# Second attention of a decoder layer: values kept transposed, sums inverted by way of DRAM, weighed on GpSimd, packed for the output product by DMA

## What is computed

```python
def _L0_xattn_ref(x, cross_input, ...):        # H = 16 heads of D = 16
    ...
    y = einsum('bhqk,bhkd->bhqd', softmax(att), v)          # causal, over x
    y = y + einsum('bhqk,bhkd->bhqd', softmax(attc), vc)    # over the context
    y = y.transpose(0, 2, 1, 3).reshape(B, T, C)
    return y @ Wp + bp
```

## Time and profile before

| | |
|---|---|
| median of 3 runs | 1285.73 us (1284.77 to 1291.07) |
| the profiled execution's own time | 1284.18 us |
| its span, first to last instruction | 1282.5 us |
| TensorE busy | 1180.3 us, 92% |
| VectorE busy | 924.3 us, 72% |
| ScalarE busy | 821.3 us, 64% |
| GpSimd busy | 499.1 us, 39% |
| mean granted TensorE clock | 0.982 |

### The profile page before, as it was taken

How to read it: one execution, slowest core, us unless ns; L and a number is a source line. 1 busy time by engine, 2 the same in 40 slices (tenths; PEclk the granted TensorE clock), 3 DMA queues, 4 the chain that set the end, 5 groups by cost and what they waited for, 6 DMA issues and landing times.

```text
span 1282.5 us, 25128 instructions
## 1 busy us (share of the span) xinstructions
PE 1180.3 (92%) x8870; PEld 535.9 (42%) x8870; DVE 924.3 (72%) x2376; ACT 821.3 (64%) x1577; POOL 499.1 (39%) x519
## 2 busy tenths in 40 slices
PE   6799999999999999868899988888888999999998
PEld 2233434444444444234333233322333266666666
DVE  3777777777777777767788787778877467656564
ACT  3566666666666666634677766676666677667663
POOL 0267878888777788914212111131111130000000
PEclk9999999999999999988999999999999899999999
DMA  7534333322333332021121221112100522232300
GB/s 226 169 101 120 101 83 94 99 81 80 82 83 84 84 81 83 12 71 42 48 80 43 65 61 42 43 53 72 42 26 1 197 97 102 80 135 100 115 17 17
DMA packets 82482, 103.00 MB, mean 80 GB/s; under 512 B 12626, under 2 KB 74066, under 8 KB 82326
## 3 DMA queue, kind: packets, MB, share of 16 engines
q1 hardware_dynamic: 81174, 100.87, 26.9%
q10 hardware_dynamic: 160, 0.39, 0.1%
q0 software_dynamic: 1024, 0.13, 0.1%
HBM read 65.37 MB, written 10.68 MB: 59 GB/s over the span
## 4 chain that ended last, share of the span: by engine, by line
PE 75%; DVE 14%; ACT 5%; issue 4%; DMA 1%; POOL 1%; ACTq 0%; SPq 0%; DVEq 0%; POOLq 0%
PE a_s L1301 10%; PE a_o L466 9%; DVE a_mx L1609 8%; PE a_m L1287 7%; PE a_o L1220 6%; PE a_a L409 6%; PE a_s L456 5%; PE a_s L457 4%; PE a_m L1175 4%; PE a_e L506 3%; PE a_a L419 3%; PE a_m L432 3%; PE a_a L166 3%; PE a_s L1202 3%; PE a_s L1287 2%
## 5 line engine op out<-in xcount | busy, mean ns | idle before, releaser
L1609 DVE TENSOR_REDUCE a_mx<-a_m 128x1 f32<-128x512 f32 (+3 forms) x512 | 271.4, 583 | 77.7 <-PE a_m L1175 68.6
L1434 ACT ACTIVATE a_pt<-a_s 128x512 f32<-128x512 f32 (+3 forms) x512 | 235.0, 515 | 113.9 <-PE a_s L1202 111.5
L637 ACT ACTIVATE a_pt<-a_s 128x512 f32<-128x512 f32 x256 | 149.6, 597 | 167.0 <-DVE a_s L764 138.7
L755 DVE CUSTOM_DVE_ANT_0 a_junk<-a_m,a_rtile 128x512 f16<-128x512 f32 x256 | 167.2, 687 | 0.7 <-issue 0.7
L846 POOL TENSOR_TENSOR a_ps<-a_ps,a_pt 128x512 f32<-128x512 f32 x128 | 159.6, 1268 | 1.0 <-ACT a_pt L637 1.0
L466 PE MATMUL a_o<-a_pt,a_v 128*64 128x512 f32 x512 | 140.0, 625 | 2.6 <-DVE a_a L769 2.5
L1855 POOL TENSOR_SCALAR_AFFINE_SELECT a_pt<-a_pt 128x512 f32<-128x512 f32 x64 | 40.8, 637 | 226.5 <-ACT a_pt L1434 226.5
L764 DVE TENSOR_TENSOR a_s<-a_s,a_near 128x218 f32<-128x218 f32 (+1 forms) x256 | 107.9, 433 | 14.5 <-PE a_s L457 11.6
L456 PE MATMUL a_s<-a_q,a_k 128*128 128x512 f16 x256 | 99.2, 388 | 7.6 <-ACT a_pt L637 6.2
L744 DVE TENSOR_TENSOR a_nat<-a_a,a_nat 128x512 f16<-128x512 f32 x64 | 44.3, 692 | 83.7 <-ACT a_nat L612 83.7
L846 POOL TENSOR_TENSOR a_ps<-a_pt 128x512 f32<-128x512 f32 x64 | 80.0, 1270 | 55.5 <-ACT a_pt L637 55.5
(11 more groups left out here) (295 smaller groups left out, 2606.5 us busy)
## 6 DMA issues: line engine op xcount, KB each, us to landing
a_rtile<-lines SPq DMA_DIRECT2D x32, 448.0 KB, 3.9
a_q<-a_nat SPq DMA_DIRECT2D x192, 64.0 KB
a_k<-a_nat SPq DMA_DIRECT2D x192, 64.0 KB
a_vy<-in_Wa SPq DMA_DIRECT2D x12, 1024.0 KB, 4.9
a_vy<-in_Wb SPq DMA_DIRECT2D x12, 1024.0 KB, 7.3
a_qk<-halves SPq DMA_DIRECT2D x40, 128.0 KB, 2.7
halves<-a_held SPq DMA_DIRECT2D x16, 256.0 KB, 2.3
halves<-a_held SPq DMA_DIRECT2D x32, 128.0 KB, 2.4
```

The source lines that it names most:

```text
L637: act.activation(pt[:, n % RING, ::-1], bank_s[j % 2][:, :], ACT.Exp, scale=SC1 / QS).then_inc(sm["act_s"], 1)
L755: dve.tensor_tensor_reduce(junk[h][:, :], bank_m[h][:, :], rtile[:, u % 3, h, qb * P:qb * P + S], -1 / MAXROW, 3e38, ALU.add, ALU.min, mx[ ...
L1434: act.activation(pt[g % 4][:, h, first:], bank_s[(32 * u + j) % 3][:, first:], ACT.Exp, scale=SC2 / QS).then_inc(sm["act_s"], 1)
L1609: dve.tensor_reduce(mx[u % 2][:, qb, to:to + 1], bank_m[j % 3][:, 0:keys], AX.X, ALU.max).then_inc(sm["dve_b"], 1)
```

## The change

The copy of the bank stays transposed all the way. Each unit's eight rows of sums (4 heads, 2 halves, 512 queries) go to DRAM (`sums2`), come back as 128 x 32 (`total_of`), are inverted by one VectorE instruction, go to DRAM again (`inverses2`) and come back spread, each row of 512 to 32 partitions (`inv`). GpSimd then multiplies the two halves, adds them and adds the bias: four instructions of 128 x 512. Four DMAs pack the 64 value rows of the unit into `yts`. The two transposes and their copies are gone. SP carries these DMAs for units 0 to 14 and POOL those of unit 15. Buffers: `osb` three deep, `y`, `ys`, `r` gone.

```diff
-        CROSS, SELF, MAX, ROWS_AT, SCORE, VALUE, COPY, TURN, ADD = -13, -9, 16, 33, 38, 42, (49, 57), (61, 63), 64
+        CROSS, SELF, MAX, ROWS_AT, SCORE, VALUE, COPY, INVERT, WEIGH = -13, -9, 16, 33, 38, 42, (49, 57), 64, 70
+        OPS = 4
...
+        def of_unit(u, name, n=1):
+            return (sm[f"last_{name}"], n * DMA) if u == UNITS - 1 else (sm[name], n * DMA * (u + 1))
+        flat_row = [[2 * G2 * S // P, P], [1, 2 * G2 * S // P]]
+        def gather(engine, u):
+            if u < 0:
+                return
+            engine.wait_ge(sm["act_o"], 2 * u + 2)
+            for x in range(2):
+                engine.dma_start(sums2[u, x], osb[u % 3][x][D2:P:2 * D2, :]).then_inc(of_unit(u, "sums_out")[0], DMA)
+            engine.wait_ge(*of_unit(u, "sums_out", 2))
+            if u > 0:
+                engine.wait_ge(sm["dve_r"], u)
+            engine.dma_start(total_of[:, :], bass.AP(sums2.tensor, u * 2 * G2 * S, flat_row)).then_inc(of_unit(u, "sums_in")[0], DMA)
+        def spread_inverse(engine, u):
+            if u < 0:
+                return
+            engine.wait_ge(sm["dve_r"], u + 1)
+            engine.dma_start(bass.AP(inverses2.tensor, u * 2 * G2 * S, flat_row), inv_of[:, :]).then_inc(of_unit(u, "inv_out")[0], DMA)
+            engine.wait_ge(*of_unit(u, "inv_out"))
+            if u > 0:
+                engine.wait_ge(sm["pool_y"], OPS * u)
+            for x in range(2):
+                engine.dma_start(inv[x][:, :], bass.AP(inverses2.tensor, (2 * u + x) * G2 * S, [[S, G2], [0, 2 * D2], [1, S]])
+                                 ).then_inc(of_unit(u, "inv_in")[0], DMA)
+        def pack(engine, u):
+            if u < 0:
+                return
+            b, g = divmod(u, GROUPS)
...
+            if u > 0:
+                engine.wait_ge(*of_unit(u - 1, "packed", G2))
+            engine.wait_ge(sm["pool_y"], OPS * u + OPS)
+            for h in range(G2):
+                o = g % 2 * CG + h * D2
+                engine.dma_start(yts[b][o:o + D2, g // 2, :], osb[u % 3][0][h * 2 * D2:h * 2 * D2 + D2, :]
+                                 ).then_inc(of_unit(u, "packed")[0], DMA)
 
         def sync(sp):
...
                 store_self(sp, second, halves2, u)
+                gather(sp, u - 4)
+                pack(sp, u - 5)
+                spread_inverse(sp, u - 4)
...
+            for u in range(UNITS - 4, UNITS - 2):
+                gather(sp, u)
+                pack(sp, u - 1)
+                spread_inverse(sp, u)
             sp.wait_ge(sm["pe_o"], 8 * (UNITS - GROUPS))
-            sp.wait_ge(ps["act_y"], KC * (LATE + 1))
             for u in range(UNITS_E):
                 i = u % 2
+                if u == 2:
+                    gather(sp, UNITS - 2)
+                    pack(sp, UNITS - 3)
+                    spread_inverse(sp, UNITS - 2)
+                if u == 3:
+                    pack(sp, UNITS - 2)
...
             def product_y(b, i, to):
-                pe.wait_ge(ps["act_y"], KC * (b + 1))
+                pe.wait_ge(*of_unit(b * GROUPS + GROUPS - 1 - b // (B - 1), "packed", G2))
+                if b == B - 1:
+                    pe.wait_ge(*of_unit(UNITS - 1, "packed", G2))
...
-                    if (slot, n) == (2, 4):
-                        pe.wait_ge(sm["dve_y"], 2 * UNITS)
-                        turn_y(LAST, 0, bank_a)
-                    if (slot, n) == (2, 5):
-                        turn_y(LAST, 1, bank_o)
-                    if (slot, n) == (2, 8):
+                    if (slot, n) == (3, 1):
+                        pe.wait_ge(sm["act_rows"], UNITS)
                         product_y(LAST, 0, bank_a)
-                    if (slot, n) == (2, 9):
+                    if (slot, n) == (3, 2):
                         product_y(LAST, 1, bank_o)
...
             def out_of_bank(u, x):
                 act.wait_ge(sm["pe_o"], 8 * u + 4 * x + 4)
-                if u > 0:
-                    act.wait_ge(sm["pe_t"], 2 * u + x - 1)
-                act.activation(osb[x][:, :], bank_o[:, :], ACT.Copy).then_inc(sm["act_o"], 1)
+                if u > 2:
+                    act.wait_ge(*of_unit(u - 3, "packed", G2))
+                act.activation(osb[u % 3][x][:, :], bank_o[:, :], ACT.Copy).then_inc(sm["act_o"], 1)
...
-            def weigh(u, x):
...
+            def invert(u):
+                dve.wait_ge(*of_unit(u, "sums_in"))
                 if u > 0:
-                    dve.wait_ge(sm["pool_y"], u)
...
+                    dve.wait_ge(*of_unit(u - 1, "inv_out"))
+                dve.reciprocal(inv_of[:, :], total_of[:, :]).then_inc(sm["dve_r"], 1)
...
+                    if (slot, n) == (2, 6):
+                        invert(UNITS - 1)
...
+            def weigh(u, step):
+                o = osb[u % 3]
+                pool.wait_ge(*of_unit(u, "inv_in", 2))
+                if step < 2:
+                    ins = pool.tensor_tensor(o[step][:, :], o[step][:, :], inv[step][:, :], ALU.mult)
+                else:
+                    pool.wait_ge(sm["pool_y"], OPS * u + step)
...
+                    if step == 2:
+                        ins = pool.tensor_tensor(o[0][:, :], o[0][:, :], o[1][:, :], ALU.add)
+                    else:
+                        ins = pool.tensor_scalar(o[0][:, :], o[0][:, :], vb[:, u % GROUPS:u % GROUPS + 1], None, ALU.add)
+                ins.then_inc(sm["pool_y"], 1)
...
+                u, i = unit_at(n, WEIGH, 2 * OPS)
+                if u is not None and u < UNITS - 1 and i % 2 == 0:
+                    weigh(u, i // 2)
...
+            gather(pool, UNITS - 1)
+            spread_inverse(pool, UNITS - 1)
+            for step in range(OPS):
+                weigh(UNITS - 1, step)
+            pack(pool, UNITS - 1)
```

More of the change, by code:

```diff
@@ L999, in order_of_bank_a @@
             for n in CLOCK:
-                for x in range(2):
-                    u, i = unit_at(n, TURN[x])
-                    if u is not None:
-                        yield "turn", 2 * u + x
                 for name, first, least in (("cross", CROSS, 2), ("self", SELF, 1), ("rows", ROWS_AT, 0)):
@@ L1035, in attention_2_and_experts @@
         before = dict(zip(uses[1:], uses))
[L1036 to L1037 removed]
+        emptied = {"cross": sm["dve_cross"], "self": sm["dve_self"], "rows": sm["act_rows"],
+                   "product": ps["dve_w"], "turn x": ps["dve_lo"]}
         def bank_a_free(pe, name, i):
@@ L1315, in tensor @@
                     make(n - FILL)
-                for x in range(2):
-                    u, i = unit_at(n, TURN[x])
-                    if u is not None:
-                        turn_back(u, x)
                 u, i = unit_at(n, CROSS, 2)
@@ L1768, in vector @@
                     make(n - FILL)
-                for x in range(2):
-                    u, i = unit_at(n, TURN[x])
-                    if u is not None:
-                        weigh(u, x)
+                u, i = unit_at(n, INVERT)
+                if u is not None and u < UNITS - 1:
+                    invert(u)
                 u, i = unit_at(n, SELF + 2)
```

105 lines of the change are left out of this document (33 added, 72 removed).

## The result

The changed kernel takes 1328.35 us (median of 4 runs, 1325.08 to 1332.04) against 1287.1 us for the kernel before on the same chip: a ratio of 1.032, 95% interval 1.028 to 1.036. The profiled execution took 1326.7 us, its span is 1325.0 us, 42.5 us more than before. I had forecast 1288 with a range up to 1306: the time lies outside it, on the slow side.

A forecast was written before the change was run, and what follows sets the result against it. TensorE and VectorE were taken to alternate in the attention and TensorE alone to bound the expert stage: 1284.2 - 14 + 17 = 1287.2, with the median 1.5 us above the profiled execution, given as 1288; range 1271 to 1306.

The forecast's parts named there:

- The gain of the removed work: Attention: transposes, reciprocals and products removed, less a new reciprocal, leave 15.6 us, taken as 14; ends 7 and 20.
- I charge nothing in the steady state: Attention units: the spread lands in 3 to 7 us, GpSimd's triangle is ready in time, so no cost.
- rival 2: Attention: the spread lands late in every unit, `pv` waits about 2 us 15 times, 30 us, 1318 in all; chance 0.13.
- the turns as pure cost: Attention: two `turn_back` of four transposes a unit removed from TensorE, 1.4 us a unit, 6.8 us on the chain.
- Rival 4: Something else, as a clock falling in more places because TensorE has gaps; either side, no size given; chance 0.05.
- the loss at the passage, 17 us: Passage to the experts: 15.4 us of hole in TensorE's list and 1.6 us of clock restart; ends 10.4 and 26.
- The hole before the last product: Expert stage: values packed at 1051 against a product able to start at 1035.6, 15.4 us; sign 12 to 22 us.
- Its cover: SP in each attention unit: free at 908.5, next work the moves at 915.34, so 7 us cover the added wait.
- the units were to be 0.9 us shorter: Attention, sign in the profile after: distance between VectorE's once-a-unit rows shorter by about 0.9 us; wrong if units keep their length.
- Rival 1: Passage to the experts: the tail is hidden, packing ends near 1037, only the steady gain is left, 1273; chance 0.17.
- Rival 3: Attention: TensorE's wait for banks replaces the transposes, only 4 us come out, 1299 in all; chance 0.15.

The follow-up runs named there:

- e1: The changed kernel with the spread as eight transfers of 32 outermost rows in place of two: 1316.16 us, ratio 1.024 to the kernel before.
- e8: The changed kernel with the spread as eight transfers and eight unused transposes a unit where the removed ones stood: 1299.82 us, ratio 1.011 to the kernel before.
- e9: The changed kernel with e1, e4 and e8 together (wide spread, later last product, unused transposes): 1272.02 us, ratio 0.989 to the kernel before.
- e5: The kernel before with only the spread added, as two narrow transfers into a buffer that nobody reads: 1290.64 us, ratio 1.005.
- e11: The changed kernel, its spread left narrow, with the eight unused transposes a unit of e8: 1323.79 us, ratio 1.028 to the kernel before.
- e7: The kernel before with one of four blocks transposed in each turn of the attention's output, no transfer added: 1298.65 us, ratio 1.012.
- e10: The changed kernel with e1 and e4 together, without the unused transposes: 1292.91 us, ratio 1.005 to the kernel before.
- e4: The changed kernel with the last product one slot later in the expert stage, unit 15's inversion and what follows moved too: 1305.16 us, ratio 1.016 to the kernel before.
- e13: e10 with eight unused transposes a unit in one row ahead of the self projection: 1303.68 us, ratio 1.015 to the kernel before.
- e6: The kernel before with only the spread added, as eight transfers of 32 outermost rows into an unread buffer: 1286.43 us, ratio 1.000.

## Why the prediction was wrong

**The gain of the removed work had about the right size; its terms were not those that I gave.** I took 14 us out, ends 7 and 20, which is 0.9 us a unit. Where the clock is full and the spread wide, the units are 1.0 us shorter (140.5 to 134.3 us for six, e1), and over the attention e8 is 11.7 us shorter, e9 11.6. But `turn_back` had 6.8 of my 18.1 us by its share of the chain, and e8, which has the transposes on TensorE again, is as fast in these units as e1 without them. What TensorE no longer did was worth nothing there; the gain came of the rest of the turn. That the total fits is in part luck.

**First failed step: "I charge nothing in the steady state".** It rested on the spread's landing of 3 to 7 us. It measures 8.0 to 10.4. I had the bound from transfers with many partitions on both sides and had the Trainium skill's rule against it beside me; I used the rule only to choose the end of the range. And I looked for the victim in the wrong place. I followed the spread to its own readers, as rival 2 did: GpSimd's multiplication, the triangle, `pv`. GpSimd's multiplications do wait (76 us in all between 640 and 1020), and nothing follows from it: `pv`'s weight loads wait 2.6 us in all for the triangle, and waited 2.7 before. The one that waits is score, 8.3 us in weight loads, for a 4 KB transfer issued by another engine 0.6 us behind the spread. The prediction lists what is queued behind every new wait on an engine, and not what shares the DMA engines with the new transfer. This is worth 12 us as the kernel stands (e1), 6 in the kernel before (e5), 24 with the unused transposes in (e8, e11).

**Second failed step: the turns as pure cost.** "Each unit loses two `turn_back`" was priced by what TensorE no longer does. What it also no longer does is be at work among its short waits. Rival 4 named it, a clock that falls in more places because TensorE has gaps, and gave it 0.05 and no price. Measured alone (e7) three quarters of the removal cost 14 us; in the changed kernel with the spread wide, all of it costs 16 us (e8 against e1), or 21 with the tail mended (e9 against e10). The row was there to be read: in the earlier trace rows TensorE had 14 of 100 us idle at 0.97, and the earlier trace rows showed the clock at 0.50. I took that as a matter of the passage.

**Third failed step: the loss at the passage, 17 us, measures 30.5.** The hole before the last product was forecast as 15.4 us, 17 with the clock. It measures 19.05 us, within the 12 to 22 that I gave as a sign, and its place and releaser are as told. What I put at nothing are two more places: `turn_x` waits 6.5 us for GpSimd's scaling, and `downward` 3.3 us for a `low` that stands behind `invert` of unit 15: with the hole 28.9 of the 30.5 us. The hole itself fits because two delays nearly cancel: TensorE reaches the product at 1049, not 1035.6, and the last values are packed at 1068.1, not 1051. Of the 17 us of the packing, 12.3 are the late second copy of unit 14. Of the rest, two terms were too short: GpSimd weighs unit 14 beside VectorE's splits in 8.2 us, not 5.6 (the multiplications 1.7 us each, the addition 2.07, the bias 2.33), and the spread of unit 15 is in 10 us after its issue, not 3 to 7. Unit 15's weighing took the 5.6 us that were its lower bound. Moving the product by one slot takes 23 us off (e4), 23 with the spread wide (e10 against e1) and 28 with the unused transposes (e9 against e8).

**Smaller terms.** `invert` takes 0.345 us, not 0.25, within the bounds; it waits 3.2 us for unit 15 as well as 11.5 for unit 14. GpSimd's bias addition takes 1.56 us (1.8 taken). SyncE has ten new issues a unit, not thirteen (three in `gather`, three in `spread_inverse`, four in `pack`). Its cover was misread: its next work behind the spread is not the moves at 915.34 but, in every second unit, a store of the context's halves, which the kernel before has at

```profile
912.26 1.23 SPq L181 DMA_DIRECT2D halves<-a_held  x2
```

so 4 us were there by my layout and not 7. They were enough: in the unit shown SyncE had issued the spread by 912.2 and made this store at 916.97. And 1287.2 with 1.5 us to the median is 1288.7, which I wrote as 1288.

**The signs and the rivals.** The hole came; but the units were to be 0.9 us shorter, and they are 0.7 us longer in the mean (386.6 against 376.1 us for 15): one of my signs of being wrong. Rival 1, a hidden tail, did not come. Rival 2 had the landing (its threshold was 9 us, the median is 9.2) and the wrong victim. Rival 3, an alternation that is not relieved, is refuted by the six units at full clock. What made the result was rival 4 with rival 2's transfer, and a passage with more places than I had.

What stays open: why the clock falls at some of these waits and not at others of the same length (up to its eighth once-a-unit row e1 has a clock of 1.00, without the transposes), and which of the things that went with the turns gives the 1.0 us a unit.

## What to carry to other kernels

Before taking work from TensorE, look at what stands between its waits: work that fills gaps may cost nothing and hold the clock up (e8), and the same work at the one other place that was tried was a loss (e13). A new large transfer has to be looked at beside every small one that is in flight at the same moment on any queue, and its outermost dimension kept large on both sides: 32 rows cost nothing here where 4 did (e5, e6). Where a chain of transfers is added ahead of an in-order consumer, move the consumer by the whole chain, measured with the queue that it will find there.

## What the runs showed that I had not expected

- Eight unused transposes a unit, 112 in all with 19.6 us of busy time in e8, make the kernel 16 to 21 us faster (e8 against e1, e9 against e10).
- At full clock these transposes cost nothing: six units take 134.3 us with them and without.
- A single wait of 1.5 us of TensorE was followed by 10 us at the 1.2 GHz level.
- A transfer of 4 KB on GpSimd's queue took up to 5.4 us to land beside transfers of 256 KB with four outermost rows on SyncE's, against 3.3 us at most before.
- The changed kernel with three edits, a wide spread, a later last product and the unused transposes, is 1.1% faster than the kernel before (e9).
